# A fused convolution and feed-forward block: maxima over the partitions by VectorE's transposes, gelu and its high parts in one step, and a new split of the last steps

## What is computed

```python
x = x + dwconv7x7(ln_over_channels(x), w_sym)         # w_sym: mean of the 4 rotations
t = tokens(x)                                          # 16 x 1024 tokens of 192 channels
# quantize(y): for each of 5 groups of 3 images: gamma = max |y| of the group,
#   clip(y * 128 / (gamma + eps), -128 + eps, 128 - eps); the 16th image is in no group and gives 0
h = gelu(quantize(ln(t) @ sign(W1).T + b1))            # 768 hidden values
out = t + quantize(h @ sign(W2).T + b2)
```

## Time and profile before

| | |
|---|---|
| median of 3 runs | 638.99 us (636.84 to 643.13) |
| the profiled execution | 639.97 us |
| its span, first to last instruction | 638.1 us |
| busy: TensorE, VectorE, ScalarE, POOL | 507.2, 456.3, 393.7, 201.6 us |
| mean granted TensorE clock | 0.912 of 2.4 GHz |

### The profile page before, as it was taken

How to read it: one execution, slowest core, us unless ns; L and a number is a source line. 1 busy time by engine, 2 the same in 40 slices (tenths; PEclk the granted TensorE clock), 3 DMA queues, 4 the chain that set the end, 5 groups by cost and what they waited for, 6 DMA issues and landing times.

```text
span 638.1 us, 9846 instructions
## 1 busy us (share of the span) xinstructions
PE 507.2 (79%) x3552; PEld 355.9 (56%) x3552; DVE 456.3 (72%) x1041; ACT 393.7 (62%) x626; POOL 201.6 (32%) x193
## 2 busy tenths in 40 slices
PE   2357348999899977667699899989998999868683
PEld 2346348999899973233255455645554565435452
DVE  7988741222278987976799789797988798656655
ACT  2698930000001347668999799968999698948730
POOL 4000100000300000000476747484666467525430
PEclk9776768999999986879999899989999899969987
DMA  7997335666955639600111000221132333413345
GB/s 218 297 338 199 87 85 146 165 175 171 232 161 153 173 141 399 234 0 1 50 51 51 8 18 23 79 92 57 50 100 75 101 123 100 175 49 100 100 149 173
DMA packets 55280, 81.29 MB, mean 127 GB/s; under 512 B 7361, under 2 KB 39105, under 8 KB 55232
## 3 DMA queue, kind: packets, MB, share of 16 engines
q1 hardware_dynamic: 39616, 68.28, 34.9%
q10 hardware_dynamic: 15136, 11.22, 6.2%
q0 software_dynamic: 480, 1.17, 0.9%
HBM read 53.12 MB, written 27.53 MB: 126 GB/s over the span
## 4 chain that ended last, share of the span: by engine, by line
PE 45%; ACT 23%; DVE 14%; DMA 8%; issue 6%; SPq 3%; ACTq 0%; DVEq 0%
PE bank L969 18%; ACT arena L561 7%; PE bank L1051 6%; ACT arena L555 6%; DMA arena<-x 5%; DVE am L841 4%; PE bank L1061 4%; DMA arena<-kz_d 3%; PE bank L1019 3%; PE bank L1020 3%; PE bank L1021 3%; ACT arena L568 2%; PE bank L992 2%; ACT arena L467 2%; DVE arena L763 2%
## 5 line engine op out<-in xcount | busy, mean ns | idle before, releaser
L420 POOL TENSOR_TENSOR arena<-arena 128x512 f16<-128x512 f32 x159 | 183.1, 1189 | 265.7 <-DVE arena L828 232.0
L555 ACT ACTIVATE arena<-bank,b1s 128x512 f32<-128x512 f32 x180 | 124.7, 705 | 44.4 <-PE bank L1021 44.0
L969 PE MATMUL bank<-arena 128*128 128x112 f32 (+1 forms) x1152 | 135.9, 282 | 18.5 <-ACT arena L467 12.0
L969 PEld LDWEIGHTS bank<-arena 128*128 128x128 f32 x1152 | 134.8, 199 | 19.4 <-ACT arena L467 12.2
L1051 PE MATMUL bank<-arena 128*128 128x512 f16 x360 | 107.6, 394 | 1.7 <-ACT arena L579 1.7
L561 ACT ACTIVATE arena<-arena,gm 128x1024 f32<-128x1024 f32 x90 | 102.9, 1165 | 8.0 <-DVE gm L863 8.0
L841 DVE TENSOR_REDUCE am<-arena 128x1 f32<-128x3072 f32 x30 | 100.3, 3345 | 2.3 <-ACT arena L555 2.3
L1019 PE MATMUL bank<-arena 128*128 128x512 f16 x180 | 72.1, 401 | 23.1 <-ACT arena L555 11.8
L747 DVE TENSOR_TENSOR arena<-bank,arena 128x512 f32<-128x512 f32 x48 | 33.2, 691 | 79.0 <-PE bank L969 78.9
L482 ACT ACTIVATE arena<-arena,wmean 51x576 f16<-51x576 f32 (+1 forms) x10 | 8.6, 856 | 127.0 <-DVE wmean L721 114.3
L1020 PE MATMUL bank<-arena 128*128 128x512 f16 x180 | 71.3, 396 | 0.0
(11 more groups left out here) (118 smaller groups left out, 662.1 us busy)
## 6 DMA issues: line engine op xcount, KB each, us to landing
arena<-park_d SPq DMA_DIRECT2D x44, 384.0 KB, 3.6
arena<-kz_d SPq DMA_DIRECT2D x100, 112.0 KB, 2.9
arena<-kz_d ACTq DMA_DIRECT2D x92, 112.0 KB, 3.4
park_d<-arena SPq DMA_DIRECT2D x6, 1536.0 KB, 14.5
arena<-x SPq DMA_DIRECT2D x8, 1024.0 KB, 9.1
out<-arena SPq DMA_DIRECT2D x32, 256.0 KB, 2.0
kz_d<-arena SPq DMA_DIRECT2D x8, 672.0 KB, 9.5
arena<-x SPq DMA_DIRECT2D x16, 256.0 KB, 9.5
```

The source lines that it names most:

```text
L420: last = pool.tensor_tensor(out=low_half(u, m, m + 1), in0=yslot(u)[:, 2 * m:2 * m + 2, :], in1=hib(u, m, m + 1), op=ALU.subtract)
L555: act.activation(yslot(s)[:, 2 * m:2 * m + 2, :], m1p[c % 2][:, :].rearrange("p (h n) -> p h n", h=2), ACT.Identity, bias=b1s[:, m:m + 1], ...
L969: last = t.matmul(ps[:, :, lo:hi], WB[BUFS[g]][:, 1 - db, c, :], xn[:, :, lo + db:hi + db], start=(db == 0), stop=(db == -1))
```

## The change

- The largest value over the partitions no longer goes through TensorE. `over_all` on VectorE writes the maximum of the six columns 32 times side by side, transposes four 32x32 blocks so that all 128 values lie along each of 32 partitions, and reduces these for each quarter of the partitions. `as_row`, `to_all`, `over_row` and their waits on TensorE go.
- `LAGA` becomes 7, so gelu lags seven steps; `LAGH` stays 7, so the high parts are made in the step of their gelu. ScalarE does the gelu parts in the order 1, 2, 0 after the evictions 0, 1 and 3, and its `high` after evictions 4 and 5. No step has the gelus in one lump. VectorE's `high` waits for two of the three gelu parts only.
- `HA` becomes 3: ScalarE copies three parts, VectorE casts three, POOL subtracts the latter three and then the former three.
- VectorE's order becomes (`over_all(1)`, `scale2` in `first2` steps), `final`, `largest`, `high`, `token_low`, (`over_all(0)`, `scale` in `first` steps; in step 30 they stand ahead of `high`), `normal`, `largest2`.
- The tail: `HL` = 2 and `LP` = (2, 5). ScalarE copies parts 0 and 1, VectorE casts the other four; POOL subtracts parts 2 to 4 and waits for VectorE's cast in place of ScalarE's copy; VectorE subtracts part 5 and parts 0 and 1. TensorE's order of parts is 5, 2, 3, 4, 0, 1, and its `x_back` stands behind `upper` (`bring_turned`). ScalarE evicts both results, then does the gelus, then `high`.

```diff
-LAGA = GT
-LAGH = LAGA + 1
+LAGA = GT + 1
+LAGH = LAGA
...
-HA, HL, LP = 2, 4, 3
+HA, HL, LP = 3, 2, (2, 5)
...
+ORDER = {False: (*range(HA, MT), *range(HA)), True: (*range(LP[1], MT), *range(*LP), *range(LP[0]))}
+
+PARTS = (1, 2, 0)
...
             for u in range(LAST, FT):
-                pool.wait_ge(hiA, u + 1)
-                low(u, 0, LP)
+                pool.wait_ge(hiV, u + 1)
+                low(u, *LP)
...
+                    if m in (0, 1, 3) and 0 <= u < FT:
+                        gelus(u, PARTS[(0, 1, 3).index(m)])
...
+                    if m == 4 and 0 <= k < FT:
+                        high(k, 0, 2)
+                    if m == 5 and 0 <= k < FT and ha(k) > 2:
+                        high(k, 2, ha(k))
...
-                dve.wait_ge(gelu, 3 * (u + 1))
+                dve.wait_ge(gelu, 3 * u + 2)
...
+            def over_all(k, g, values, counted, done):
+
+                dve.wait_ge(counted, g * GT)
+                v.tensor_reduce(SQ, values[:, :].rearrange("p (o g) -> p o g", o=1).to_broadcast([P, 32, GT]), AX.X, ALU.max) \
+                    .then_inc(sqr[k], 1)
+                dve.wait_ge(sqr[k], g)
+                for q in range(4):
+                    v.transpose(TQ[:, 32 * q:32 * q + 32], SQ[32 * q:32 * q + 32, :]).then_inc(gtr[k], 1)
+                dve.wait_ge(gtr[k], 4 * g)
+                for q in range(4):
+                    v.tensor_reduce(gm[32 * q:32 * q + 32, 6 * k:6 * k + 1], TQ, AX.X, ALU.max).then_inc(done, 1)
...
+                if first2:
+                    over_all(1, g2, am2, amx2, gall2)
+                    scale2(g2)
+                if 0 <= s - LAGF < FT:
+                    final(s - LAGF)
+                if 1 <= s <= FT:
                     largest(s - 1)
-                    if 0 <= s - LAGF < FT:
-                        final(s - LAGF)
-                    over_row(0, g)
+                if s == FT:
+                    over_all(0, g, am, amx, gall)
+                    scale(g)
+                if 0 <= s - LAGH < FT:
+                    high(s - LAGH)
+                if 0 <= s + 1 < FT:
+                    token_low(s + 1)
+                if first and s < FT:
+                    over_all(0, g, am, amx, gall)
+                    scale(g)
                 if s > 5 and s + 2 < FT:
                     normal(s + 2)
-                if not first and 0 <= s - LAGH < FT:
-                    high(s - LAGH)
...
-                    if first and m == 2:
-
-                        pe.wait_ge(f15, 4)
-                        if s >= LAGF:
-                            pe.wait_ge(fin, min(FT, s - LAGF + 1))
-                        as_row(0, gmx, g)
-                    if first and m == 3:
-                        to_all(0, gall, g)
...
+                    if m == 4 and 0 <= v and s < FT:
+                        bring_turned(v)
                 if 0 <= u < FT:
                     upper(u)
+                if s >= FT and v < early[0]:
+                    bring_turned(v)
```

125 lines of the change are left out of this document (43 added, 82 removed).

## The result

The changed kernel takes 664.19 us (median of 6 runs, 654.26 to 666.75), the kernel before 639.45 in the same job. The ratio is 1.035, 95% interval 1.030 to 1.040: slower; it compares the fast executions alone, for the changed kernel 654.26, 662.16 and 663.25, since the other three lie more than 1.5% above the shortest. The forecast was 644, with a range of 618 to 655. The profiled execution, 654.26, is the shortest of the six.

A forecast was written before the change was run, and what follows sets the result against it. It took ScalarE, at 9.47 us a step, to bound the kernel before. Main loop +20.0 and tail -15.2 made net +4.8: 644.8 us for such an execution, 644 against the median, range 618 to 655.

The forecast's parts named there:

- ScalarE +0.48, plain steps 9.95: Main loop: one more `high` copy on ScalarE adds 0.48 us to its 9.47 a step, making 9.95.
- The late state: From step 13: `normal` lies under POOL's run and costs 4.46 us; VectorE's step becomes 10.8, with `final` 11.8, never catching up.
- The maximum, taken 2.8: Group steps: `over_all` with `scale` costs VectorE 2.8 us, from bounds of 2.1 to 3.2.
- Start to E: Main loop from the start of step 8 to E: 256.2 us against 236.2 before, so +20.0.
- E: The moment the last eviction of hidden products is handed over, where the tail begins; 553.05 us in the kernel before.
- The tail, -15.2 forecast: From E to the last `final`: 64.4 us against 79.6 before.
- the loop through POOL: Tail: gelus, cast, POOL, products, `upper` and result take 12.1 us over two steps, 6.1 a step against 7.32.
- P: Tail: time of POOL's three subtractions within the loop, taken as 4.4 us from bounds of 3.4 to 5.0.
- Half clock: Tail rival: TensorE stays at 1.2 GHz, three passages cost 3.4 us more each; 654 us, chance 0.20.
- Half the price: Main-loop rival: two of four scalings escape POOL in each of 15 late steps, 24 us less; 620 us, chance 0.18.
- catching up: Main-loop rival: `normal` fits between POOL's operations, steps stay at 9.95 to 10; 608 us, chance 0.12.

The follow-up runs named there:

- experiment 1: The changed kernel with VectorE's `normal` ahead of `high` and `token_low` instead of behind them: 619.48 us, ratio 0.972 to the kernel before.
- experiment 3: The changed kernel with each POOL subtraction cut to 8 of its 512 columns, TensorE reading the high part again: 607.47 us, ratio 0.954 to the kernel before.
- experiment 2: The kernel before with only `normal` moved behind `token_low`: 639.79 us, ratio 1.005 to the kernel before.
- experiment 6: experiment 1 with ScalarE's extra copy undone, two high parts instead of three: 637.14 us, ratio 0.997 to the kernel before.
- experiment 5: The changed kernel with `normal` ahead of the first layer's maximum and `scale` in steps 6, 12, 18 and 24: 662.96 us, ratio 1.038 to the kernel before.

## Why the prediction was wrong, by its own steps

- **ScalarE +0.48, plain steps 9.95: right.** Steps 8 to 12 are 9.95 to 9.98, and ScalarE is busy throughout steps 8 to 11.
- **The late state: right in mechanism and nearly in size.** From step 13 on VectorE is never idle, four scalings take 4.65 (4.46 forecast), a step 10.88 without `final` (10.8) and 11.92 with it (11.8). TensorE waits for POOL and for `token_low`. I had not named the turn of the tokens, which waits 16.9 for `normal`; VectorE, which never idles, would set the step without it. Experiments 1 and 3 show that `normal` under POOL's run is the cause.
- **The maximum, taken 2.8: too small.** It is 3.31 in step 12 and adds 3.5 in each step with the second layer's (15.42 to 11.92) and 1.65 in steps 18 and 24 (1.4 forecast). The range ended at 3.2. The last bound came from 0.28 for each of nine instructions; the four reductions of 128 values take 0.30 from start to start and the first one, of 192 values, 0.37. By the Trainium skill (VectorE: DVE Perf Modes, "Two Vector instructions with no wait between them") instructions whose input or output begins in another quadrant (a group of 32 partitions) than before do not overlap. The rows agree: four transposes of 0.20 fill 0.90, and four reductions of 0.28 fill 1.20. The forecast weighed that rule and took the lower number, 2.8; that was worth 0.5 in step 12.
- **Start to E, +20.0 forecast, +25.7 measured.** The terms: `high` of step 13 done 1.1 later, step 14 by 0.1 and step 15 by 0.8 longer, thirteen steps by 0.12 each (1.6), steps 21 and 27 by 0.7 each (1.4), steps 18 and 24 by 0.25 each (0.5), and 0.2 behind them.
- **The tail, -15.2 forecast, -5.1 measured: this is the step that failed.** Gelu 24 came at E + 7.5 (7.8 forecast), gelu 25 at 19.1 (16.3), gelu 29 at 48.2 (40.3), and behind gelu 29 it was 26.3 (24.1; the terms given add up to 23.7). The term that failed is the loop through POOL, 12.1 for two steps, and with it the assumption that nothing but this loop sets the tail. From gelu 24 to 26, 25 to 27, 26 to 28 and 27 to 29 the loop took 18.4, 12.8, 17.1 and 16.3. Three things stand in the 10.1. First, P: 4.99, where I took 4.4 from bounds of 3.4 to 5.0. I let VectorE's subtraction slow POOL's, but not the reverse; the pair takes 2.94, and about 2.0 when POOL's operations are short (experiment 3). The cast takes 1.40 instead of 1.22 where it meets POOL. The chain of work that ended last goes through three of POOL's runs (from 580.24, 604.21 and 624.83), 0.6 longer each: 1.8. Second, VectorE's own queue, which the forecast left out. Cast, pair, `largest2` and `final` take 6.0 from cast to cast (602.91 to 608.88), about the 6.1 of the loop, so a cast often waits for VectorE and not for its gelus: that of half-image 24 starts at 584.91, though its gelus were done at 581.8. No slack is left for the second layer's maximum in step 33, which I priced only at the end: its 3.4 delay the cast by about 2.7 (gelu at 598.06 and two gelus of 1.07 done at 600.2, cast at 602.91). Third, the clock: two passages of ten products, both on that chain, took 1.65 longer each, 3.3. These make 7.8; the rest, 2.3, I have not divided.
- **The rivals.** *Half clock*, chance 0.20, came in small part: not through the whole tail, for the 24 `upper` products read 1.52 or 1.53 each time, but twice, behind the longest waits for POOL. *Half the price* and *catching up* did not occur by themselves; catching up is what experiment 1 makes happen, at 619.5, where I had worked out 608 with a tail of 64.4. Its time with the tail as measured would be 618.
- **The sum.** 5.7 + 10.1 = 15.8 more than the 644.8 forecast for an execution like the one of before, 660.6. The median is 664.2; the last 3.6 I can't place, since no profile of a typical execution of the changed kernel exists.
- **The range.** It ended at 655 because it let one unknown at a time go to its end. The maximum at its upper end (5 times 0.5), P at its upper end and the clock all came together, and all of them lengthen the same chain of work.

## What to carry to other kernels

When VectorE's cast starts a run of GpSimd and a scaling of VectorE follows, count the distance between the two against the length of the run: 2.2 against 6.8 cost 38 us over 21 steps (experiment 1), 6.8 against 6.8 left the main loop as long as it was (experiment 2). An order that is cheap on time can be dear when late; price the late state by itself, and if its step is longer than that of the bounding engine, one delay decides the rest of the loop. Where two engines block each other, price both directions. And before a loop through several engines is taken as the bound, add up the queue of each engine in it: here VectorE's was as long as the loop.

## What the runs showed of the hardware that was not expected

- The blocking is lopsided in one case and mutual in the other. Scalings (tensor and scalar operands) beside POOL's run: POOL's six take 6.80 to 6.85 with four scalings beside them and 6.75 with none (the run at 561.43), while each scaling reads 1.21 instead of 0.37. Subtractions on both engines: POOL's three go from 3.41 (at 569.08, beside no subtraction) to 4.99 and VectorE's pair from about 2.0 to 2.94. The Trainium skill (SBUF — State Buffer, "Who interferes with whom") has the instruction that issues first hold up the other engine's for its whole length, whichever engine it is on. The scalings agree on VectorE's side; on POOL's side the six grow by 0.1 at most, which no run here explains.
- TensorE's granted clock fell for single stretches inside a busy tail (0.86 over 12 us), behind waits of 3.6 in which its last work had been turn-backs and two products. A shorter wait does not decide it either way: behind 2.41 for POOL in the same tail ten products took 2.38, at full speed, while behind 2.42 in experiment 6 and 2.43 in experiment 5, after the same turn-backs and two products, they took 4.03 and 3.95.
